# An attention and expert feed-forward kernel: the second feed-forward in pairs of 128-row tiles instead of single 256-row tiles

## The reference

```python
router_logits = xf @ gate_w
topk_vals, topk_idx = jax.lax.top_k(router_logits, TOP_K)
topk_w = jax.nn.softmax(topk_vals, axis=-1)
comb = comb.at[jnp.arange(n_tokens)[:, None], topk_idx].add(topk_w)
h = jax.nn.gelu(jnp.einsum('nd,edf->enf', xf, W1) + b1[:, None, :], approximate=False)
y = jnp.einsum('enf,efd->end', h, W2) + b2[:, None, :]
out = jnp.einsum('ne,end->nd', comb, y)
```

## Time and profile before

| what | us |
|---|---|
| time, median of 3 runs (lowest, highest) | 470.97 (469.65, 473.82) |
| span of the profiled execution, first to last instruction | 469.0 |
| median time less that span | 1.97 |
| last DVE operation of the sort's parts (`locate`) ends | 355.4 |
| first matmul of the tile stage | 372.96 |
| last matmul of the tile stage starts | 446.91 |
| last store of a tile's result has landed | 453.95 |

### The profile page before, as it was taken

One profiled execution on the slowest core, in us unless ns is written; L12 is line 12 of the kernel. 1 busy time (PEld: TensorE's weight loads), 2 busy tenths in 40 slices (PEclk: granted clock), 3 DMA queues, 4 the chain that ended last, 5 costly groups with the idle time before them and its releaser, 6 DMA issues.

```text
span 469.0 us, 12672 instructions
## 1 busy us (share of the span) xinstructions
PE 372.3 (79%) x4442; PEld 264.0 (56%) x4442; DVE 345.2 (74%) x983; ACT 268.4 (57%) x595; POOL 267.7 (57%) x342
## 2 busy tenths in 40 slices
PE   5677988987579999999987999887642399999910
PEld 3444665656236666566554666656432188888910
DVE  6775688787858786888676477878755199999906
ACT  3564677776246555565576667676411176776604
POOL 8950477676665558595830244387757226755640
PEclk9896799799579999999998599898755599999975
DMA  7286990000001111110014000000101222332127
GB/s 208 54 239 186 386 352 8 3 2 3 1 1 46 46 48 45 46 46 1 1 26 68 4 1 3 2 25 25 36 29 54 70 66 85 88 87 82 42 73 234
DMA packets 30836, 33.13 MB, mean 71 GB/s; under 512 B 3908, under 2 KB 22606, under 8 KB 30776
## 3 DMA queue, kind: packets, MB, share of 16 engines
q1 hardware_dynamic: 27692, 26.11, 19.2%
q0 software_dynamic: 2496, 5.18, 3.2%
q10 hardware_dynamic: 588, 1.05, 0.6%
HBM read 15.22 MB, written 15.01 MB: 64 GB/s over the span
## 4 chain that ended last, share of the span: by engine, by line
PE 49%; DVE 14%; POOL 13%; issue 10%; ACT 8%; DMA 4%; SPq 1%; POOLq 0%; ACTq 0%; DVEq 0%
PE ps L1249 10%; PE ps L1251 9%; PE ps L1250 9%; PE ps L1418 5%; POOL sorted_rows L712 4%; PE ps L1339 4%; DVE area L934 2%; PE ps L1370 2%; PE ps L1313 2%; POOL expert_sums L758 2%; POOL area L738 1%; PE ps L1548 1%; DMA keys<-expert_sums 1%; ACT vals L417 1%; PE ps L1364 1%
## 5 line engine op out<-in xcount | busy, mean ns | idle before, releaser
L738 POOL TENSOR_TENSOR area<-area 128x512 f16<-128x512 f32 x44 | 50.9, 1157 | 34.4 <-ACT area L538 34.3
L758 POOL DMA_INDIRECT expert_sums<-area x46 | 45.3, 985 | 39.8 <-ACT area L557 31.3
L1249 PE MATMUL ps<-w,area 128*128 128x128 f16 (+1 forms) x360 | 63.8, 219 | 0.9 <-POOL area L738 0.8
L1249 PE MATMUL ps<-area,w 128*128 128x512 f16 (+1 forms) x180 | 61.1, 339 | 3.9 <-DVE area L1135 3.1
L1250 PE MATMUL ps<-w,area 128*128 128x128 f16 (+1 forms) x360 | 63.8, 219 | 0.0
L1251 PE MATMUL ps<-w,area 128*128 128x128 f16 (+1 forms) x360 | 63.7, 219 | 0.0
L934 DVE TENSOR_REDUCE area<-ps 128x8 f32<-128x512 f32 x64 | 41.2, 686 | 26.8 <-PE ps L1418 26.4
L1250 PE MATMUL ps<-area,w 128*128 128x512 f16 (+1 forms) x180 | 60.8, 338 | 0.0
L1251 PE MATMUL ps<-area,w 128*128 128x512 f16 (+1 forms) x180 | 60.8, 338 | 0.0
L534 ACT ACTIVATE area<-ps 128x512 f32<-128x512 f32 x44 | 26.2, 597 | 38.4 <-PE ps L1548 37.8
L1339 PE MATMUL ps<-ident,area 128*128 128x128 f32 x256 | 44.5, 329 | 1.1 <-ACT area L470 1.1
(11 more groups left out here) (222 smaller groups left out, 1047.2 us busy)
## 6 DMA issues: line engine op xcount, KB each, us to landing
sorted_rows<-filler_rows SPq DMA_DIRECT2D x16, 528.0 KB, 6.2
w_stage<-in_L_ffn_W SPq DMA_DIRECT2D x8, 512.0 KB, 3.9
w<-sorted_rows SPq DMA_DIRECT2D x23, 132.0 KB
keys<-area SPq DMA_DIRECT2D x32, 48.0 KB
area<-in_ctx SPq DMA_DIRECT2D x4, 256.0 KB, 3.7
x_res<-in_x SPq DMA_DIRECT2D x4, 256.0 KB, 4.8
keys<-expert_sums SPq DMA_DIRECT2D x4, 256.0 KB, 5.5
keys<-expert_sums ACTq DMA_DIRECT2D x4, 256.0 KB, 6.0
```

The source lines that it names most:

```text
L738: nc.gpsimd.tensor_tensor(hid[:, n % 4, 1, :], gated[:, n % 4, :], hid[:, n % 4, 0, :], ALU.subtract).then_inc(q["lo"], 1)
L758: nc.gpsimd.indirect_dma_start(out=expert_sums, out_offset=bass.IndirectOffsetOnAxis(ap=to_row[:, j, h:h + 1], axis=0), in_=ys[j % OUTS][: ...
L1249: pe.matmul(dst, lhs[0], rhs[0], start=start, stop=False, **kw)
```

## The change

The tile becomes 128 rows, each with its own expert, and two of them are handled together as a pair: 39 tiles in 20 pairs, of which the last is a single tile (`halves`). Twelve full tiles (six pairs) come from a first table, made from the counts after token tile 9 (`early_counts`, `early_tiles`, `early_rows` in the attention's steps 13, 14 and 15); the others come from `late_table`, which DVE runs after it has handled pair 0, with the softmax shares (`shares`) behind it. The first six pairs wait for the indirect DMAs of token tiles 0 to 9 alone (semaphore `sa`), the others for the rest (`sc`). Token tile 8 is now stored in step 16.

In PE's program each half of a pair has its own expert register: `up` runs its `three` for each half with 128 moving columns (24 matmuls for a full pair instead of 12 of 256 columns), and `down` forms the address of `W2` for each half. ACT's Gelu runs for each half with its own bias column, eight operations of 128 columns. SP reads two row numbers and issues two loads per pair. The bias columns come in two parts (`first_biases`). What is left out below are constants' positions in `table`, the shortened filler copy, and the same renaming in further waits.

```diff
-ST = 256
-MT = 23
+ST = 128
+PAIR = 2 * ST
+EARLY = 10
+MT0 = 12
+MT1 = 28
+MT = MT0 + MT1
+NP0 = MT0 // 2
+NP = MT // 2
+LAST = NP - 1
 LOADS = 4
 OUTS = 8
 FILLS = 16
-SORT_PARTS = ((0, 4), (4, 8), (8, 10), (10, 12), (12, 14), (14, 15), (15, 16))
-TABLE = 192
+SORT_PARTS = ((0, 4), (4, 8), (8, EARLY), (EARLY, 12), (12, 14), (14, 15), (15, 16))
...
-        b1_now = sb("b1_now", [P, STEPS1, MT], F32)
...
+        b1_now = w_stage[:, 1, 0:STEPS1 * MT].rearrange("p (f j) -> p f j", f=STEPS1)
...
+        def halves(j):
+
+            return range(1) if j == LAST else range(2)
+
+        def width(j):
+
+            return ST * len(halves(j))
+
+        def rows_loaded(j):
+
+            return 16 * sum(len(halves(i)) for i in range(j % LOADS, j + 1, LOADS))
+
+        def rows_stored(n, before=NP):
+
+            return 16 * sum(len(halves(i)) for i in range(n, before, OUTS))
...
-            rows = [sp.value_load(row_i[0:1, j:j + 1], min_val=0, max_val=EXPERTS * SLOTS) for j in range(LOADS)]
-            sp.wait_ge(q["sc"], 2 * 16 * TILES)
-            for j in range(MT):
+            rows = [[first_row_of(j, h) for h in halves(j)] for j in range(LOADS)]
+            sp.wait_ge(q["sa"], 2 * 16 * EARLY)
+            for j in range(NP):
+                if j == NP0:
+                    sp.wait_ge(q["tbl"], 5)
+                    sp.wait_ge(q["sc"], 2 * 16 * (TILES - EARLY))
                 if j >= LOADS:
                     sp.wait_ge(q["slots_ps"], j - LOADS + 1)
                     sp.wait_ge(q["gate"], j - LOADS + 1)
-                    rows.append(sp.value_load(row_i[0:1, j:j + 1], min_val=0, max_val=EXPERTS * SLOTS))
-                row = rows[j]
-                sp.dma_start(slots32[:, j % LOADS, :, :].bitcast(U32), sorted_rows[bass.ds(row, ST), :].rearrange("(p h) w -> p h w", h=2)).then_inc(LD[j % LOADS], 16)
+                    rows.append([first_row_of(j, h) for h in halves(j)])
+                for h in halves(j):
+                    sp.dma_start(slots32[:, j % LOADS, h, :].bitcast(U32), sorted_rows[bass.ds(rows[j][h], ST), :]).then_inc(LD[j % LOADS], 16)
...
+                def first_biases(part):
+
+                    t0, t1 = ((0, MT0), (MT0, MT))[part]
+                    act.wait_ge(q["b1_ps"], part + 1)
+                    if part == 1:
+                        act.wait_ge(q["down"], NP0 - 3)
+                    nc.scalar.activation(b1_now[:, :, t0:t1], ps[:, (3, 6)[part], PAIR:PAIR + STEPS1 * (t1 - t0)].rearrange("p (f j) -> p f j", f=STEPS1),
+                                         ACT.Copy).then_inc(q["b1"], 1)
...
+                            for h in halves(j):
+                                r = slice(f * PAIR + h * ST, f * PAIR + h * ST + ST)
+                                mm = nc.scalar.activation(act_f[:, n % 4, r], ps[:, n % 4, r], ACT.Gelu,
+                                                          bias=b1_now[:, 2 * u + f, 2 * j + h:2 * j + h + 1], scale=1 / WSCALE)
+                        mm.then_inc(q["act"], 1)
+                    if j + 2 < NP:
                         slots_high(j + 2)
+                    if j == NP0 - 2:
+                        first_biases(1)
...
-                    if l == 1 and TILES // 2 <= t < TILES:
+                    if l == 1 and TILES // 2 <= t <= TILES:
...
+                                                 in_=rows32[:, t, :].bitcast(U32), in_offset=None).then_inc(q["sa"] if t < EARLY else q["sc"], 16)
...
-            for t in range(TILES // 2, TILES):
+            for t in range(TILES // 2 + 1, TILES):
                 scatter(t)
-            for j in range(MT):
+            for j in range(NP):
                 pool.wait_ge(q["gate"], j + 1)
                 pool.wait_ge(q["y"], j + 1)
-                for h in range(2):
+                for h in halves(j):
...
+                if t == EARLY + 3:
+                    early_counts()
+                if t == EARLY + 4:
+                    early_tiles()
+                if t == EARLY + 5:
+                    early_rows()
...
-                tile_table(q)
...
+            def whole_tiles(into):
+
+                q = F[1]
+                nc.vector.tensor_tensor(spans, counts.unsqueeze(2).broadcast_to([P, EXPERTS, 16]),
+                                        multiples.unsqueeze(1).broadcast_to([P, EXPERTS, 16]), ALU.is_gt).then_inc(q["rk"], 1)
+                dve.wait_ge(q["rk"], next(rank_steps))
+                nc.vector.tensor_reduce(into, spans, axis=AX.X, op=ALU.add).then_inc(q["rk"], 1)
+                dve.wait_ge(q["rk"], next(rank_steps))
+
+            def last_tiles(number):
+
+                q = F[1]
+                nc.vector.tensor_tensor(spans8, upto, number.unsqueeze(1).broadcast_to([P, EXPERTS, EXPERTS]), ALU.mult).then_inc(q["rk"], 1)
+                dve.wait_ge(q["rk"], next(rank_steps))
+                nc.vector.tensor_reduce(ends, spans8, axis=AX.X, op=ALU.add).then_inc(q["rk"], 1)
+                dve.wait_ge(q["rk"], next(rank_steps))
+
+            def tile_experts(t0, n):
+
+                q = F[1]
+                nc.vector.tensor_tensor(passed[:, 0:n, :], over_t(tile_id[:, 0:n], n), over_e(ends, n), ALU.is_ge).then_inc(q["rk"], 1)
+                dve.wait_ge(q["rk"], next(rank_steps))
+                nc.vector.tensor_reduce(tile_e[:, t0:t0 + n], passed[:, 0:n, :], axis=AX.X, op=ALU.add).then_inc(q["rk"], 1)
+                dve.wait_ge(q["rk"], next(rank_steps))
+                nc.vector.tensor_scalar(expert_i[:, t0:t0 + n], tile_e[:, t0:t0 + n], EXPERTS - 1.0, None, ALU.min).then_inc(q["tbl"], 1)
+
+            def tile_rows(t0, n, step):
+
+                q = F[1]
+                nc.vector.tensor_tensor(weighed[:, 0:n, :], passed[:, 0:n, :], over_e(step, n), ALU.mult).then_inc(q["rk"], 1)
+                dve.wait_ge(q["rk"], next(rank_steps))
+                nc.vector.tensor_reduce(tile_n[:, 0:n], weighed[:, 0:n, :], axis=AX.X, op=ALU.add).then_inc(q["rk"], 1)
+                dve.wait_ge(q["rk"], next(rank_steps))
+                nc.vector.scalar_tensor_tensor(tile_n[:, 0:n], tile_n[:, 0:n], -float(ST), tile_first[:, 0:n], ALU.mult, ALU.add).then_inc(q["rk"], 1)
+                dve.wait_ge(q["rk"], next(rank_steps))
+                nc.vector.scalar_tensor_tensor(tile_row[:, 0:n], tile_e[:, t0:t0 + n], float(SLOTS), tile_n[:, 0:n], ALU.mult, ALU.add).then_inc(q["rk"], 1)
+                dve.wait_ge(q["rk"], next(rank_steps))
+                nc.vector.tensor_scalar(row_i[:, t0:t0 + n], tile_row[:, 0:n], first_done if t0 else 0.0, float(EXPERTS * SLOTS),
+                                        ALU.add, ALU.min).then_inc(q["tbl"], 1)
+                nc.vector.tensor_scalar(own_e[:, t0:t0 + n], tile_e[:, t0:t0 + n], EXPERTS - 1.0, lane, ALU.min, ALU.is_equal).then_inc(q["tbl"], 1)
+
+            def early_counts():
+
+                q = F[1]
+                nc.vector.scalar_tensor_tensor(counts, bases[:, 1, :], 1.0 - ST, first_row, ALU.add, ALU.subtract).then_inc(q["rk"], 1)
+                dve.wait_ge(q["rk"], next(rank_steps))
+                nc.vector.memset(done[:, EXPERTS:EXPERTS + 1], 0.0).then_inc(q["rk"], 1)
+                dve.wait_ge(q["rk"], next(rank_steps))
+                whole_tiles(tiles_of)
+
+            def early_tiles():
+
+                q = F[1]
+                last_tiles(tiles_of)
+                nc.vector.tensor_tensor(begin, ends, tiles_of, ALU.subtract).then_inc(q["rk"], 1)
+                dve.wait_ge(q["rk"], next(rank_steps))
+                tile_experts(0, MT0)
+
+            def early_rows():
+
+                q = F[1]
+                nc.vector.tensor_scalar(begin, begin, float(MT0), None, ALU.min).then_inc(q["rk"], 1)
+                dve.wait_ge(q["rk"], next(rank_steps))
+                nc.vector.scalar_tensor_tensor(done[:, 0:EXPERTS], ends, float(MT0), begin, ALU.min, ALU.subtract).then_inc(q["rk"], 1)
+                dve.wait_ge(q["rk"], next(rank_steps))
+                nc.vector.tensor_tensor(done_step, done[:, 1:EXPERTS + 1], done[:, 0:EXPERTS], ALU.subtract).then_inc(q["rk"], 1)
+                dve.wait_ge(q["rk"], next(rank_steps))
+                nc.vector.tensor_scalar(first_done, done[:, 0:1], float(ST), None, ALU.mult).then_inc(q["rk"], 1)
+                dve.wait_ge(q["rk"], next(rank_steps))
+                tile_rows(0, MT0, tiles_of)
...
+                whole_tiles(tiles_of)
+                nc.vector.tensor_tensor(left, tiles_of, done[:, 0:EXPERTS], ALU.subtract).then_inc(q["rk"], 1)
+                dve.wait_ge(q["rk"], next(rank_steps))
+                nc.vector.tensor_tensor(begin, left, done_step, ALU.subtract).then_inc(q["rk"], 1)
+                dve.wait_ge(q["rk"], next(rank_steps))
+                last_tiles(left)
+                tile_experts(MT0, MT1)
+                tile_rows(MT0, MT1, begin)
...
+                    if j == 0:
+                        late_table()
+                        shares()
...
```

(78 more changed lines are left out.)

113 lines of the change are left out of this document (55 added, 58 removed).

## The result

The kernel after takes 502.13 us (median of 4 runs, 499.28 to 504.43), the kernel before beside it 472.39 us (4 runs). The ratio is 1.0629, 95% interval 1.0575 to 1.0683: slower by about 30 us. The prediction was 500.3 us, range 484 to 508. The profiled execution has a span of 499.6 us, 30.6 more than before.

A forecast was written before the change was run, and what follows sets the result against it. PE's sequencer was taken to bound the stage, which grows from 74 to 116 us against a 10.4 us head start and 2 us at the end: +29.3, span 498.3, plus 1.97 to the median: 500.3 us, range 484 to 508.

The forecast's parts named there:

- The bound: PE's sequencer in the stage: 17 register steps, number load and semaphore steps sum to 3.1 us against a 3.18 us period.
- The steady pair: Two expert halves per pair: 34 register steps instead of 17, two number loads instead of one; 6.0 us, from 3.18 per tile.
- What lies beside it at no cost: Per pair: array 3.0 us, DVE 3.0, POOL 2.5, ACT 2.6 to 4.5, SP's second load; all hidden under 6.0.
- Attention's delay: Early table's 20 DVE operations in attention steps 13 to 15 delay the path 3.6 us, bounds 2 and 4.8.
- The first matmul: Start of the stage: first matmul at 362.6 instead of 372.96, a head start of 10.4 us.
- The late table: DVE's 16 operations and 3 shares after pair 0, 5.0 us, cost 0.4 us; no PE wait above 1 us.
- Blocks 3 to 19: From pair 3 at 376.0, 16 more blocks of 6.0 less one number load put pair 19's `up` at 471.3.
- the rest of PE's work: After 471.3, groups of 8, 18, 18 and 9 sequencer steps take 7.4 us; PE ends at 478.7.
- The tail: Pair 19's single store waits for pair 18's two on POOL, starts at 481.0, lands at 483.2; before, 453.95.
- B: Array or DVE keeps the pace, extra address work hidden or not emitted per half: 455.2 us, chance 0.10.
- C: Steps cheaper than taken, ACT's Gelus set the pace at 4.9 us per pair: 484.4 us; chance 0.08 with D.
- D: Only half of the added steps, one half's addresses kept in registers: 4.9 us per pair, 484 us; chance 0.08 with C.

The follow-up runs named there:

- Experiments 2 to 5: 2; then the kernel before with one more number load per tile that nothing uses, 481.74 us; then experiment 4 and experiment 5.
- 2: experiment 1 with a second load of the same expert number and a separate register and address for each half in `up` and `down`; 531.89 us.
- experiment 1: Kernel before with `up` in 24 matmuls of 128 columns and eight Gelus per tile, still one expert number and address for both halves; 475.20 us.
- experiment 9: Changed kernel with the late table moved right behind the sort instead of behind pair 0; 500.65 us in one run.
- experiment 4: Changed kernel with both halves of a pair using the first half's expert in `up` and `down`, one number load per pair; 459.00 us.
- experiment 5: Changed kernel with the first half's expert used for both halves in `down` only, both numbers still loaded; 481.65 us.
- experiment 7: Changed kernel without pairs: single 256-row tiles with one expert, first five from an early table, late table behind tile 0; 470.09 us against 472.16, ratio 0.9953.
- experiment 8: experiment 7 with the late table moved right behind the sort instead of behind tile 0; 462.08 us against 471.61 for the kernel before, ratio 0.9784.

## Why the prediction was right

- **The bound** (register steps, read from the gaps on "issue", the 46 ns steps that follow each other every 0.13 us, and their sum): right. Experiments 2 to 5 show it; 2 differs from 1 only in the second register (its load, its steps) and in the order of the matmuls in `up`.
- **The steady pair**, 5.96 worked out and 6.0 taken: 6.03 measured. Number load 0.65, measured by itself 0.65; a step 0.125, measured 0.124 to 0.135.
- **What lies beside it at no cost** (DVE, POOL, ACT, SP's second load): right. DVE, ACT and POOL each had some 30 us or more idle in 60, and between 380 and 470 us no wait for a load's landing shows. ACT was busy for 28.63 / 60 x 6.03 = 2.9 us a pair, inside the bounds of 2.6 and 4.5.
- **Attention's delay**: the term was a little small, 3.6 against 4.0 in this trace and up to 4.5 in the others; the bounds 2 and 4.8 held it. (20 operations at 0.2 are 4.0, not the 4.1 written; the 3.6 was a choice below either.)
- **The first matmul**, 362.6 forecast, 364.53 measured. Of the 1.9 us some 0.5 are the attention's term and 1.3 the stretch ahead of step 13, which differs between executions of the same code; it is the largest single miss. From the end of the sort on, the forecast path held: 3.5 us to the first matmul where 3.6 were forecast, the last of them PE's two number loads for pair 1 at 363.1 and 363.8.
- **The late table**: 0.4 us, measured 0.4. Pair 3 was to come 13.4 us behind the first matmul, and came 13.6 behind. One sign that was to speak against the forecast did appear: PE's wait there is put down to DVE and is 1.23 us, over the 1 us allowed. But experiment 9, without the table there, shows 1.24 on "issue" at the same place: nearly all of it is the sequencer's own pace, so the limit of 1 us was set too low.
- **Blocks 3 to 19**: 95.35 us forecast, 472.59 - 378.12 = 94.5 measured; **the rest of PE's work**: 7.4 against 479.5 - 472.6 = 6.9.
- **The tail**: the last store was to start 2.3 us behind PE's end and started 2.8 behind it, at 482.36 instead of 481.0.

The misses of +1.9, +0.2, -0.9, -0.5 and +0.6 leave 1.3, and the span is 499.6 instead of 498.3. So the total is nearer than the terms, partly by luck: +1.3 of the first miss is the stretch that varies between executions, and opposite signs cancel.

Of the rivals, B was a real price for a kernel without the steps (455.2 by its sum, 459.0 in experiment 4); it didn't occur because the steps are emitted for each half. Its "table, now bare" appears there too: the wait of 4.62 us at pair 3. C had an ACT period of 4.9; ACT is busy for half of the pair. D's time (484) is met by experiment 5, which has about half of the added steps (481.65).

The rule weighed, some 81 ns for each sustained load and matmul of 128 columns (the Trainium skill, TensorE: Matmul & The Clock Gate, Back-to-back issue gap), is at odds with experiment 1: 50 of them in a tile would take 4.05 us, and the whole tile took 3.24. For the steps another page fits: the Trainium skill (Perfetto Trace Analysis, Sequencer-only Instruction) says that the profiler reports only the execution of such an instruction, not its semaphore wait or propagation. The trace agrees: 46 ns are shown, 125 ns pass. What fills the other 79 ns no run here shows.

## What to carry to other kernels

An address that depends on a run-time number is paid on PE's sequencer, 0.125 us each; in this kernel that was the bound. Count distinct run-time addresses per tile, multiply by the distance between their starts (not by the duration shown), and compare the sum with the period before splitting work into pieces that each have a number of their own. Where two pieces can share an address (one expert for 256 rows), sharing it is worth more here than the fewer, fuller tiles that the split gives. And when a computation is moved off the start of a stage, look for the gap in which its engine already waits: put a few positions earlier, the same 4 us of work were free.

## What was not expected

- The 4.3 us stall of experiment 7 cost more than itself. Between the same marks the traces of 7 and 8 differ by 5.4 us: 4.0 at tile 3, and 1.4 behind it, where PE's granted clock was 0.66 over 5 us (1.00 in experiment 8). The medians differ by 8.0 us, 470.09 to 462.08, in two sets of runs (their kernels before differ by 0.5); what makes the remaining 2 us or so is not shown.
- A register step costs the same, 0.12 to 0.14 us, from 17 steps a period to 34 and whether the array is full (kernel before) or has time to spare (kernel after); so it adds up in a straight line.
- A stretch of the attention took 11.2 us in six of the eleven profiled executions and 12.5 in five, with the same work in it and, in the changed kernel and experiment 9, the same code. Profiles of two kernels can differ by over 1 us ahead of any edit, so a stage is compared from a mark just in front of it.
